# A transformer block on one core: ScalarE's tables named by hand, and every engine's order of steps written anew

## The reference

```
x = L0_attn_x                                        # 16 x 512 x 256
mod = (_silu(L0_c) @ L0_wmod).reshape(16, 6, 1, -1)  # sa, ca, ga, sb, cb, gb
h = _layernorm(x) * (1 + ca) + sa
x = x + ga * attention(h)       # causal, softmax over |scores|
h = _layernorm(x) * (1 + cb) + sb
x = x + gb * ffn(h)
```

## Time and profile before

| | us |
|---|---|
| median of three runs | 478.34 (478.26 to 478.99) |
| the profiled execution | 478.56 |
| its span, first to last instruction | 476.8 |

### The profile page before, as it was taken

How to read it: one execution, slowest core, us unless ns; L and a number is a source line. 1 busy time by engine, 2 the same in 40 slices (tenths; PEclk the granted TensorE clock), 3 DMA queues, 4 the chain that set the end, 5 groups by cost and what they waited for, 6 DMA issues and landing times.

```text
span 476.8 us, 7729 instructions
## 1 busy us (share of the span) xinstructions
PE 402.6 (84%) x2080; PEld 310.6 (65%) x2080; DVE 386.1 (81%) x1383; ACT 320.6 (67%) x672; POOL 59.6 (13%) x97
## 2 busy tenths in 40 slices
PE   4999999999999998999899989997999968435220
PEld 4866786876877786769676967695777737334110
DVE  3765464688599898999899989997699987595896
ACT  2255728958994899579956996699669556835220
POOL 4112244100100030202020202001010110020132
PEclk9999999999999999999999999999899997875555
DMA  8613330023005131722262236304122430042152
GB/s 237 201 47 114 112 92 20 22 90 102 10 16 169 38 54 36 155 90 55 58 152 92 47 65 148 96 3 66 45 70 43 66 67 1 0 70 43 26 78 95
DMA packets 32906, 35.65 MB, mean 75 GB/s; under 512 B 3376, under 2 KB 28448, under 8 KB 32864
## 3 DMA queue, kind: packets, MB, share of 16 engines
q1 hardware_dynamic: 24752, 26.88, 18.7%
q0 software_dynamic: 7536, 7.48, 11.7%
q10 hardware_dynamic: 576, 0.80, 0.5%
HBM read 19.36 MB, written 15.79 MB: 74 GB/s over the span
## 4 chain that ended last, share of the span: by engine, by line
PE 66%; ACT 14%; DVE 9%; issue 8%; DMA 1%; ACTq 0%; DVEq 0%
PE bank L602 11%; PE bank L562 10%; PE bank L585 10%; PE bank L575 9%; PE bank L624 6%; PE bank L611 3%; ACT L1068 3%; PE bank L593 3%; PE bank L664 3%; PE bank L550 2%; ACT gath L1218 2%; DVE y L2029 2%; ACT xhat L1108 2%; PE bank L655 1%; ACT L1206 1%
## 5 line engine op out<-in xcount | busy, mean ns | idle before, releaser
L602 PE MATMUL bank<-v,probsT 128*128 128x257 f32 x320 | 81.3, 388 | 6.6 <-ACT gath L1218 5.2
L585 PE MATMUL bank<-h,g 128*128 128x128 f32 (+3 forms) x256 | 79.7, 439 | 3.1 <-ACT hidT L1201 3.1
L602 PEld LDWEIGHTS bank<-v,probsT 128*128 128x128 f32 x320 | 58.0, 193 | 16.5 <-ACT gath L1218 6.4
L575 PE MATMUL bank<-m_ga,h 128*128 128x258 f32 x256 | 64.7, 383 | 1.1 <-ACT h L1118 1.1
L562 PE MATMUL bank<-h,a_sb 128*128 128x512 f32 x128 | 60.2, 594 | 0.4 <-ACT gath L1218 0.4
L1745 POOL DMA_DIRECT2D out<-res x14 | 18.2, 1298 | 303.6 <-DVE res L2043 303.6
L585 PEld LDWEIGHTS bank<-h,g 128*128 128x128 f32 x256 | 43.3, 192 | 19.2 <-issue 9.1
L575 PEld LDWEIGHTS bank<-m_ga,h 128*128 128x128 f32 x256 | 46.4, 190 | 10.7 <-issue 3.6
L1858 DVE CUSTOM_DVE_ANT_0 probs<-bank,cmask 128x128 f32<-128x128 f32 (+1 forms) x64 | 30.9, 483 | 23.0 <-ACT bank L1134 22.8
L1134 ACT ACTIVATE bank<-bank,v 128x128 f32<-128x128 f32 (+1 forms) x64 | 32.0, 500 | 20.9 <-PE bank L585 19.6
L1108 ACT ACTIVATE xhat<-x,nmr,rstd 128x256 f32<-128x256 f32 x62 | 35.7, 602 | 6.8 <-DVE nmr L1823 6.8
(11 more groups left out here) (179 smaller groups left out, 836.6 us busy)
## 6 DMA issues: line engine op xcount, KB each, us to landing
x<-in_L_attn_x SPq DMA_DIRECT2D x16, 512.0 KB, 3.9
out<-x SPq DMA_DIRECT2D x14, 512.0 KB, 4.8
out<-res POOLq DMA_DIRECT2D x14, 512.0 KB, 6.5
gb_row<-gate_rows SPq DMA_DIRECT2D x16, 256.0 KB, 3.7
a_row<-gate_rows SPq DMA_DIRECT2D x14, 256.0 KB, 3.1
out<-res SPq DMA_DIRECT2D x2, 512.0 KB, 3.4
wide<-in_L_wmod SPq DMA_DIRECT2D x1, 768.0 KB, 12.1
wide<-in_L_wmod ACTq DMA_DIRECT2D x1, 512.0 KB, 5.8
```

What stands on the lines that cost most here:

```text
L575: last = mm(ps[:, 0:VW], h[s][:, c, t * P:(t + 1) * P], m_ga[p % 2][s][:, c, :], start=(c == 0), stop=(c == KC - 1))
L585: last = mm(ps[:, 0:w], g[s][:, c, t * P:(t + 1) * P], h[s][:, c, 0:w], start=(c == 0), stop=(c == KC - 1))
L602: last = mm(ps[:, 0:D + 1], probsT[s][t][:, j * P:(j + 1) * P], v_sb[s][:, j, 0:D + 1], start=(j == 0), stop=(j == t))
```

## The change

The change has two parts. The first adds a function that names the table of gelu and tanh, takes the load of the ln-exp table out of `tanh`, and puts calls of both into ScalarE's list. The gelu table stands behind the last exp ahead of a gelu or tanh, and the ln-exp table behind the last gelu or tanh of such a group:

```
@@ scalar @@
             def exp_table():
                 nc.scalar.preload_act_table_set("natural_log_exp_and_others")
+
+            def gelu_table():
+                nc.scalar.preload_act_table_set("gelu_and_others")
...
                 A(comp[g % 2][:, 0:tiles(g), :], cmp_t[:, 0:tiles(g), :], ACT.Tanh).then_inc(tanh_rdy, 1)
-                exp_table()
```

The second part writes the order of steps of all five engines and the table of banks anew. No step's own text is changed. Of the banks and of SyncE's list:

```
-            "BT2 GA1 GA5 HD S13 V11 su_ga su_vb su_wo",
+            "AT13 FS2 HD PT02 PT13 S02 S13 su_bias su_cT su_colf",
...
             ldga(6, 0)
-            ldgb(3, 0)
+            for i in range(0, 2):
+                ldgb(3, i)
             ldga(6, 1)
             ldx(6, 0)
             xo(4, 0)
-            ldgb(3, 1)
             ldx(6, 1)
             xo(4, 1)
```

On GpSimd the setup of the feed-forward constants (`sp_rest`) moves up. In the middle, `ms(p, 0)` stands ahead of both `ay` of a group instead of between them and the one before:

```
-            ay(1, 0)
             ms(6, 0)
-            ay(1, 1)
+            for i in range(0, 2):
+                ay(1, i)
             ms(6, 1)
```

More of the change, by code:

```diff
@@ L396, in _ @@
             ldga(7, 0)
-            ldgb(4, 0)
+            for i in range(0, 2):
+                ldgb(4, i)
             ldga(7, 1)
@@ new lines, in _ @@
+            for i in range(0, 4):
+                S_(2, 0, i)
+            HT(1, 0)
+            G_(2, 1, 0)
+            HT(1, 1)
+            V_(2, 1, 0)
+            HT(1, 2)
+            G_(2, 1, 1)
+            HT(1, 3)
+            FS(1, 0)
+            OHT(0, 0)
+            FS(1, 1)
+            PT_(2, 0, 0)
+            FS(1, 2)
+            PT_(2, 0, 1)
+            for i in range(0, 2):
+                GA(0, i)
+            OHT(0, 1)
+            V_(2, 1, 1)
+            GA(0, 2)
+            AT(2, 0, 0)
@@ new lines, in _ @@
+            GA(0, 3)
+            V_(2, 1, 2)
+            S_(2, 1, 0)
+            PT_(2, 0, 2)
+            for i in range(4, 7):
+                GA(0, i)
+            AT(2, 0, 1)
+            GA(0, 7)
+            S_(2, 1, 1)
+            PT_(2, 0, 3)
+            V_(2, 1, 3)
+            HD(1)
+            AT(2, 0, 2)
+            XT(3, 0, 0)
+            S_(2, 1, 2)
+            PT_(2, 1, 0)
+            BT(0, 0)
+            AT(2, 0, 3)
+            PT_(2, 1, 1)
+            S_(2, 1, 3)
@@ L1639, in _ @@
             y_gs(6)
-            for i in range(0, 2):
+            gelu_table()
+            for i in range(0, 3):
                 c_ga(7, i)
@@ new lines, in _ @@
+            for i in range(0, 2):
+                ob(0, i)
+            b_x2(3, 0, 0)
+            ob(0, 2)
+            oa(0, 6)
+            clc(2, 0)
+            a_nw(4, 0)
+            clc(2, 1)
+            b_st(3, 0, 0)
+            ob(0, 3)
+            a_nw(4, 1)
+            clc(2, 2)
+            c_b2(1)
+            ob(0, 4)
+            clc(2, 3)
+            ob(0, 5)
+            clc(2, 4)
+            a_nw(4, 2)
+            ob(0, 6)
+            oa(0, 7)
+            clc(2, 5)
@@ L3011, in _ @@
-            ob(7, 2)
+            clc(8, 1)
+            y_var(6, 1)
+            c_b2(7)
+            clc(8, 2)
+            for i in range(2, 4):
+                y_var(6, i)
+            clc(8, 3)
+            oa(6, 0)
+            clc(8, 4)
+            oa(6, 1)
+            clc(8, 5)
+            y_nw(6, 0)
+            clc(8, 6)
+            y_nw(6, 1)
+            clc(8, 7)
+            y_nw(6, 2)
+            oa(6, 2)
+            clc(8, 8)
+            oa(6, 3)
+            ob(6, 0)
+            clc(8, 9)
@@ new lines, in _ @@
+            ob(6, 4)
+            lob(8, 3)
+            y_var(7, 3)
+            lob(8, 4)
+            oh(8, 0)
+            oa(6, 6)
+            oh(8, 1)
+            ob(6, 5)
+            y_nw(7, 0)
+            oa(6, 7)
+            ob(6, 6)
+            y_nw(7, 1)
+            ob(6, 7)
+            oa(7, 0)
+            y_nw(7, 2)
+            for i in range(1, 4):
+                oa(7, i)
+            ob(7, 0)
+            spl(8, 0)
+            ob(7, 1)
+            spl(8, 1)
+            for i in range(2, 4):
+                ob(7, i)
@@ L3021, in _ @@
-            for i in range(0, 3):
                 y_var(8, i)
```

2318 lines of the change are left out of this document (1116 added, 1202 removed), and 16 rows, old and new, of the table BANK.

## The result

The changed kernel took 460.97 us, the median of four runs (460.66 to 461.63), beside 478.66 us for the kernel before in the same sitting: ratio 0.9613, 95% interval 0.9559 to 0.9668. The forecast was 466.1, its range 457 to 475. The profiled execution took 460.97 us, with a span of 459.2.

What follows compares the result with a forecast made beforehand. TensorE (84% busy) and VectorE (81%) were nearly full in the loop, with ScalarE's table loads on the path. Terms -5.2 - 2.5 - 3.6 - 2.6 - 1.5 + 1.2 + 2.0 = -12.2 us gave 466.1 us; range 457 to 475.

Steps and rivals of the forecast that it cites:

- Loop gathers: Loop over pairs: TensorE's four waits before line 602 for ScalarE's eviction of the gathers go, -5.2 us (0 to -6.4).
- Last turn's xhat: Last loop turn: all four xhat precede the gelu, so TensorE's wait at line 550 goes, -2.5 us (0 to -2.5).
- Between xhat and V: Loop: TensorE reaches V (line 575) sooner and its wait for h doubles, +2.0 us (-1.1 to +5.1).
- GpSimd's hold: Loop: GpSimd's m_ga products stretch VectorE instructions, 3.5 us a turn; where holds move unknown, counted 0 (-3.5 to +1.7 a turn).
- Rival B: Holds go too: VectorE gets 3.5 us back in three turns, TensorE bounds the loop, tail caps reached; 459 us, chance 0.12.
- Start: Kernel start: bias products moved up wait for the last bias load, a TensorE hole of +1.2 us (0 to +3).
- Tail: Groups 6 to 8: fewer table loads before gathers, -3.6 and -2.6 us; product moved behind group 8's scores, -1.5 us.
- The expectation for VectorE's gather waits: Tail: VectorE's waits for the gathers fall under 1.3 us in place of 4.87 and 3.90.
- Rival A: Loop: VectorE takes over, a turn stays 48.4 us and the 5.2 us are not earned; 471 us, chance 0.25.
- Rival D: No change: loads go, waits pass to other inputs, the rest of the tail pays for start and V; 478 us, chance 0.05.
- Rival C: Loop: x's load behind both gate-row loads goes out late and VectorE waits, +18 us; 484 us, chance 0.08.
- signs of being wrong: TensorE waits over 2 us a turn for h, VectorE waits for x, or last 87 us not 5 us shorter.

Runs made afterwards that it cites:

- the second execution: The changed kernel run once more unchanged, median 462.25 us in six runs; the traced execution meant here took 464.18 us.

## Why the prediction was right, and where it was off

The direction and the range held; the forecast was 5 us too high. That it came so near is in part luck: by the stretches above the start cost 5.5 us more than I had put, while the middle brought 4.5 us more and the tail 6.4.

*Loop gathers, -5.2:* the reason was right, the size was not. The waits for the gathers before line 602 went, but TensorE reached the next wait sooner: six loads fewer took 5.2 us of waits away and gave 2.7 us, and in the changed kernel 1.7 us for the gathers stand before line 593. I had counted four turns of 48.4 us from 107 us on; by the first g of each pair they are 42.8, 44.0, 48.5, 48.4 and 50.4 us, and only two are full ones. *Last turn's xhat, -2.5:* right, and it took with it a fall of the clock that cost 1.7 us. *Between xhat and V, +2.0:* wrong in sign; the wait fell by 0.6 us. TensorE does come to V sooner, but h is ready sooner as well. Only with 35 loads left in does it rise (2.6 us), so my caution was for the order without the loads.

*GpSimd's hold, counted 0:* the term without a size. I had read that two instructions a turn are held, 3.5 us (they are 1.92 and 2.75 us long, 0.18 and 0.6 without a product beside them, so 3.9), and named the moved list, but said that no row tells where the hold falls. It was readable: each product stood behind an output transfer that waited for VectorE's last output row, so it always began when VectorE had work; in the new list and order it waits for the landing of its gate row. Undoing the list alone costs the middle 5.1 us and the median 5.8. Rival B had the mechanism, with 1.5 us a turn; the turns' lengths don't show it so, it lies in one place.

*The middle as a whole:* my terms give -5.7, measured -10.2. TensorE's idle time and busy time add up to it. The idle time between the first g of pair 0 and that of pair 7 fell from 10.8 to 4.8 us, 6.0 us, which is what my terms were about. The busy time fell by 4.2 us, for which I had no term: 1.7 us are the fall of the clock in the last turn of the kernel before, 1.4 us are the instructions that moved into the start, 1.2 us remain. That the idle time comes out right is in part luck: with GpSimd's old list it falls to 7.8 us only, so gathers, xhat and h were worth about 3 us where I had 5.7, and the list, counted 0, the other 3. The parts don't add: six loads alone -2.7 without the clock, the list alone 0, both -6.8 by the table, or -5.1 without the clock, in the old order. The order by itself was not run, so how much it brings without the other two is open.

*Start, +1.2:* mis-sized. The hole is 2.26 us, since the last bias load took 8.5 us and not 7.7 to land. The rest of the 6.6 us to the first G step is the lower level, 2.9 us (bias products, gate row and product A take 8.8 us, 5.9 before), and 1.4 us of work moved ahead of it (the gate rows of all sequences and the signatures), which the middle no longer has. Other executions with the old setup reached the first g at 23.8, 25.9, 26.1 and 26.6 us, the last three with a granted clock under 1.00 between 20 and 28 us; so 23.5 us is one of the better ones. Against these the starts of the changed kernel (29.4 and 30.2 us) cost 3 to 6 us.

*Tail, -7.7 with caps of -10.5:* measured -14.1, or -10.2 in the second execution. VectorE's idle time in the tail fell by 11.0 us, its busy time by 3.1; in the second execution by 7.6 and 2.7. Of both, 1.6 us are the clock's fall between 390 and 400 us in the execution that I read, whose row on the granted clock I had not used. The busy time had no term. The expectation for VectorE's gather waits (under 1.3 us) held for one and not for the other (2.5 us).

*Rival A* (VectorE takes over) fell: it has 4.2 us idle a turn. *Rival D* had a part of it: some waits passed on, as the 1.7 us before line 593, but the time went down. *Rival C* fell: the gate rows go out at 226.10 us, the load of x at 240.15, no later than before (239.82), and VectorE waits for no x in a full turn. One of my signs of being wrong did come up, VectorE waiting for a load of x, 2.4 us at 61.6 us and 1.8 us at 108.2, but no gate row went out just ahead of those loads, so it isn't C's reason. Two small sums are off without changing a bound that matters: 5.2 and 1.1 are 6.3 and not 6.4, and 4.4 and 3.9 are 8.3 and not 8.8.

## What to carry to other kernels

A wait that ends on one resource can hide a second one: price an edit in the kernel that has the other edits, since here GpSimd's list brought nothing by itself and 5.8 us beside them. Where one engine holds another, look at what releases the holding instruction; if that is the held engine's own output, they collide turn after turn, as six times here between 100 and 345 us. Before a tail or a start is priced, read the granted clock of that stretch, and in more than one execution if there are more: here two falls of the clock in the traced execution of the kernel before were 3.3 us of the gain that the traces showed.

## What was not expected of the hardware

One GpSimd product beside VectorE stretches an instruction of 0.18 us to 1.92, two in a row one of 0.47 us to 3.85. TensorE's clock fell to its lower level within the first 28 us in several executions, in one from 18 to 24 us behind a wait of 1.8 us, in another from 12 to 20 us with TensorE busy in all of it; and the first products ran at half speed, to about 13 us in one execution and to 24 in another, while the granted clock read 1.00. Two executions of the changed kernel differed by 3.2 us, with lower clocks in three stretches of the tail of the longer one. Why the clock falls while TensorE is busy no run here tells.
